# Cross attention of a perceiver block: a finished tile's out-projection one slot later, its norm in the next batch's first two slots

## What is computed

```python
xn = _ln(x, g_x, b_x)              # context, 16 x 512 x 512
ln = _ln(latents, g_l, b_l)        # latents, 16 x 64 x 512
q = ln @ w_q
k, v = jnp.split(concatenate([xn, ln], axis=1) @ w_kv, 2, axis=-1)
sim = jnp.einsum('bhid,bhjd->bhij', q, k)       # 8 heads of 64
attn = jax.nn.softmax(sim, axis=-1)
out = jnp.einsum('bhij,bhjd->bhid', attn, v)
x = x + _ln(out @ w_out, g_o, b_o)
```

## Time and profile before

| | |
|---|---|
| median of 3 runs | 982.22 us (981.43 to 985.5) |
| the profiled execution's own time | 984.02 us |
| its span, first to last instruction | 982.2 us |
| granted TensorE clock | 0.998 |
| busy share: TensorE, weight loads, VectorE, ScalarE, GpSimd | 97%, 79%, 78%, 45%, 13% |

### The profile page before, as it was taken

One profiled execution on the slowest core, in us unless ns is written; L12 is line 12 of the kernel. 1 busy time (PEld: TensorE's weight loads), 2 busy tenths in 40 slices (PEclk: granted clock), 3 DMA queues, 4 the chain that ended last, 5 costly groups with the idle time before them and its releaser, 6 DMA issues.

```text
span 982.2 us, 16675 instructions
## 1 busy us (share of the span) xinstructions
PE 948.5 (97%) x6400; PEld 778.0 (79%) x6400; DVE 768.8 (78%) x1647; ACT 439.4 (45%) x848; POOL 130.7 (13%) x145
## 2 busy tenths in 40 slices
PE   9999899998999999999999999999999999999997
PEld 7778788787887887887878888777676778888885
DVE  6546588788788988987887874568898598999985
ACT  4533664655465456547545654623333422222221
POOL 6420100101110100100111110023132100000000
PEclk9999999999999999999999999999999999999999
DMA  6687675956876685676758467081003940000000
GB/s 217 186 275 178 188 128 151 188 95 188 156 132 160 145 172 120 188 140 151 134 144 197 95 169 178 1 219 30 1 2 89 261 123 12 11 11 12 12 12 22
DMA packets 119451, 120.06 MB, mean 122 GB/s; under 512 B 47430, under 2 KB 88070, under 8 KB 117324
## 3 DMA queue, kind: packets, MB, share of 16 engines
q1 hardware_dynamic: 111980, 93.30, 35.8%
q0 software_dynamic: 6816, 24.64, 14.0%
q10 hardware_dynamic: 576, 1.05, 0.3%
HBM read 89.04 MB, written 29.93 MB: 121 GB/s over the span
## 4 chain that ended last, share of the span: by engine, by line
PE 57%; DVE 21%; DMA 10%; issue 5%; ACT 5%; SPq 1%; POOL 1%; another core or an unknown queue 0%; DVEq 0%; ACTq 0%
PE ps_banks L147 14%; PE ps_banks L148 13%; PE ps_banks L149 13%; DMA scratch_rstd<-sb_rstd_b 6%; PE ps_banks L472 4%; PE ps_banks L685 3%; DVE sb_kfull L928 3%; DVE sb_kT_lo L899 3%; DVE sb_b_stats L860 2%; PE ps_banks L752 2%; PE ps_banks L753 2%; PE ps_banks L604 2%; PE ps_banks L754 2%; DMA sb_rstd_row<-scratch_rstd 2%; DVE sb_wq_big L1055 1%
## 5 line engine op out<-in xcount | busy, mean ns | idle before, releaser
L1455 ACT ACTIVATE sb_kT_hi<-sb_kfull 128x512 fp32r<-128x512 f32 x64 | 40.5, 632 | 158.6 <-DVE sb_kfull L928 158.6
L147 PE MATMUL ps_banks<-sb_zT_hi,sb_wkv_hi 128*128 128x512 f32 x256 | 104.6, 409 | 0.4 <-DVE sb_kfull L928 0.2
L148 PE MATMUL ps_banks<-sb_wkv_lo,sb_zT_hi 128*128 128x512 f32 x256 | 100.3, 392 | 0.0
L149 PE MATMUL ps_banks<-sb_zT_hi,sb_wkv_lo 128*128 128x512 f32 x256 | 100.3, 392 | 0.0
L147 PE MATMUL ps_banks<-sb_wkv_hi,sb_zT_hi 128*128 128x512 f32 x256 | 100.1, 391 | 0.0
L149 PE MATMUL ps_banks<-sb_wkv_hi,sb_zT_lo 128*128 128x512 f32 x256 | 100.1, 391 | 0.0
L148 PE MATMUL ps_banks<-sb_zT_lo,sb_wkv_hi 128*128 128x512 f32 x256 | 99.9, 390 | 0.0
L979 DVE CUSTOM_DVE_ANT_0 sb_probs<-ps_banks,sb_maskbias 128x576 f32<-128x576 f32 x64 | 48.1, 751 | 33.4 <-PE ps_banks L149 32.7
L147 PE MATMUL ps_banks<-sb_wgu,sb_z_hi 128*128 128x512 f32 (+1 forms) x192 | 73.7, 384 | 0.0
L148 PE MATMUL ps_banks<-sb_wgu,sb_z_hi 128*128 128x512 f32 (+1 forms) x192 | 72.1, 376 | 0.0
L149 PE MATMUL ps_banks<-sb_wgu,sb_z_lo 128*128 128x512 f32 (+1 forms) x192 | 72.0, 375 | 0.0
(11 more groups left out here) (269 smaller groups left out, 2425.9 us busy)
## 6 DMA issues: line engine op xcount, KB each, us to landing
sb_ctx<-in_ctx SPq DMA_DIRECT2D x16, 1024.0 KB, 6.4
sb_ctxT<-in_ctx_t SPq DMA_DIRECT2D x16, 1024.0 KB, 8.6
scratch_wgu<-sb_w_both POOLq DMA_DIRECT2D x22, 512.0 KB
sb_wgu<-scratch_wgu SPq DMA_DIRECT2D x44, 256.0 KB, 5.1
sb_wdn<-scratch_wdn SPq DMA_DIRECT2D x8, 704.0 KB, 7.8
scratch_q<-sb_a_qk POOLq DMA_DIRECT2D x8, 512.0 KB, 6.7
sb_rstd_row<-scratch_rstd SPq DMA_DIRECT2D x16, 256.0 KB, 5.4
sb_qpack<-scratch_q SPq DMA_DIRECT2D x32, 128.0 KB, 8.4
```

The costliest lines, as they stand in the source:

```text
L147: e.matmul(o, wh, xh, start=i == 0, stop=False)
L148: e.matmul(o, wh, xl, start=False, stop=False)
L149: m = e.matmul(o, wl, xh, start=False, stop=i == n - 1)
L1455: e.activation(dst, src, ACT.Identity).then_inc(done)
```

## The change

The edits hold for tiles 0 to 6. The last tile (in the round that drains the loop) keeps its slots. TensorE's `project_out` goes from slot 6 to slot 7, after the scores of that slot and ahead of its values, and ScalarE's `copy_y` goes with it. VectorE's `out_stats` goes from the end of slot 7 to the end of slot 0 of the next batch, behind `scale_k`; `out_scale` goes from there to the end of slot 1. GpSimd's `power_one` goes from slot 7 to slot 0 of the next batch, behind the spill of that slot's weight, and `shift_y` to slot 1. No work is added or removed. `out_split` and `hi_of_attn` stay. The ring's order becomes: values 1, weight, probabilities 0, latent part 0, values 2, probabilities 1, latent part 1, y, values 3.

```diff
@@ tensor_program
-                    if b % 2 == 0 and b >= 2 and slot == 6:
+                    if b % 2 == 0 and b >= 2 and slot == (7 if cur else 6):
                         project_out((b - 2) // 2)
@@ vector_program
-                    if t_new is not None and slot == 7:
+                    if t_new is not None and not cur and slot == 7:
                         o_nth = out_stats(t_new)
                     if t_out is not None:
                         if slot == 0:
+                            o_nth = out_stats(t_out)
+                        if slot == 1:
                             out_scale(t_out, o_nth)
                         if slot == 7:
                             out_add(t_out)
@@ scalar_program
-                    if t_new is not None and slot == 6:
+                    if t_new is not None and slot == (7 if cur else 6):
                         copy_y(t_new)
@@ pool_program
-                    if t_new is not None and slot == 7:
+                    if t_new is not None and b == NB and slot == 7:
                         power_one(small_o, t_new)
                     if t_out is not None:
                         if slot == 0:
+                            power_one(small_o, t_out)
+                        if slot == 1:
                             shift_y(t_out)
                         if slot == 7:
                             power_one(small_y, t_out)
```

## The result

The changed kernel takes 996.35 us (median of 4 runs, 993.28 to 998.0) against 981.98 us (4 runs, 981.43 to 985.5). The ratio is 1.0113, 95% interval 1.0086 to 1.014: slower, by 11.1 us of 982 (8.4 to 13.8). The two medians lie further apart, 14.4 us, and with four executions of each this difference stays open; the forecast misses by either. Its profiled execution took 995.66 us with a span of 993.9, which is 11.7 us more than the span before. I had forecast + 6.2 us, 988.4, and the range to 992.0 does not hold the result.

The account below looks back on a forecast made before the run. The prediction took a slack-free two-batch loop through VectorE, the statistics' round trip and TensorE as the bound. It summed + 6.35 (odd runs) - 0.7 (TensorE's wait) + 0.5 (batch 13) = + 6.2 us, 988.4 us, range 980.0 to 992.0.

Parts of the forecast that it names:

- TensorE's wait: Slot 6, even batches: of 1.06 us, 0.23 gained and 0.83 left on copy_v; 0.7 us in all, bounds 0 and 1.2.
- Slot 0 gives nothing back: VectorE, odd batches: out_stats (1.02 us) replaces out_scale (1.27), but the next low half starts at 191.80 either way.
- `power_one` was hidden: GpSimd, slot 0: power_one, behind the spill, finishes before out_scale wants it, hidden by 0.26 us.
- the drain of the weight's bank: Transposes behind the moved project_v claim the turned weight's bank: no wait, with 0.2 us to spare.
- The rival of the new bank order: Slot 7's transposes wait for the bank if VectorE is 1 us later: five times 0.8, 992.4 us; chance 0.06.
- TensorE's second tie to the loop: Slot 1, even batches: transposes wait for a weight half whose buffer a spill frees, released by VectorE in odd slot 5.
- Slot 1: + 1.27 us: VectorE, odd batches: out_scale is new before L948, adding 1.27 us; five batches give 6.35 us, bounds 5.1 and 6.35.
- `shift_y` has until slot 7: 0: GpSimd's shift_y, moved to slot 1, is not needed until slot 7, so it costs 0.
- Batch 13: 0.5 us: Its later L948 makes VectorE 1.2 to 4.5 us late in batch 14; TensorE loses 0 to 3 us, 0.5 taken.
- The loop has no slack: Two-batch loop: VectorE's odd run (15.29 us), round trip (19.32), VectorE's even batch, TensorE's slots 6 and 7; no slack.
- What closes it: The statistics' round trip from L948 to scale_k: its 12.83 us store competes with traffic that L948 itself releases.
- the context columns' earlier issue: Even batches: 1 MB of columns issued sooner may delay the row's load up to 0.8 us each; 0 taken, 1.5 for range.

Follow-up runs that it names:

- The move alone: Kernel before with only project_out of tiles 0 to 6 and its copy_y moved to slot 7, VectorE and GpSimd as before: 971.2 us, ratio 0.9981.
- the kernel with `out_scale` first: Kernel before with project_out and copy_y in slot 7, out_stats ending slot 7, and out_scale ahead of scale_k in slot 0: 970.8 us, ratio 0.9979 to before.
- `shift_y` later: Changed kernel with GpSimd's shift_y in slot 5 instead of slot 1 of the odd batch: 977.01 us, ratio 1.0047 to the kernel before.
- `shift_y` beside L1040: Kernel before with one wait added, so that GpSimd's shift_y in slot 0 waits for the second scale_k: 978.39 us, ratio 1.0053.
- norm alone: Kernel before with only VectorE's and GpSimd's part of the diff, project_out staying in slot 6: 985.55 us, ratio 1.0126.
- With it short: Dense store, dense row load and scale_k reading with a stride of four: on the kernel before 979.41 us, ratio 1.0029; on the changed one 988.11, 1.0109.
- with TensorE slower: Dense store with TensorE taking every fourth column: on the kernel before 975.4 us, ratio 1.0030; on the changed one 976.01 us, 1.0034.

## Why the prediction was wrong

The direction and the place were right. One term of the sum was put at nothing and should have been nearly as large as the whole forecast; the move's gain and batch 13 were too small, and slot 1 was too large. In the prediction's order:

*TensorE's wait.* 1.06 us became 0.83 in batch 2, as derived, to 0.01 us. The move alone is worth 0.19% or 1.8 us (0.6 to 3.0); I had 0.7, bounds 0 and 1.2, so the two can't be told apart.

*Slot 0 gives nothing back.* Right, and shown by the kernel with `out_scale` first. `power_one` was hidden, and the drain of the weight's bank did not bite. The rival of the new bank order expected TensorE to wait for it in slot 7 of even batches, and no such wait came. The 6.4 us on the same line in the changed kernel stand elsewhere, at 224.6, 365.1, 436.3 and 576.0 us, about the start of batches 4, 8, 10 and 14. That is the wait that the prediction had called TensorE's second tie to the loop. With the move alone they are absent.

*Slot 1: + 1.27 us.* Measured by `shift_y` later: 16.25 - 15.29 = 0.96 us. `out_scale` takes 196.08 - 194.90 = 1.18 there, and L1035 behind it 0.68 instead of 0.92, since `shift_y` has left its side.

**"`shift_y` has until slot 7: 0."** This step failed. I asked when its result is wanted, and not what runs beside it. It costs 0.96 us per odd batch, in L1040: six times that is 5.8 us, about half of what the change costs, where the sum had 0. Taking it away gave 0.66%, 6.4 us; adding it alone, with a run of + 0.77, cost 0.53%, 5.2 us. The trace of before held the hint: L1035 at 0.92 us beside `shift_y`, where its neighbours of the same form take 0.68. The Trainium skill, "SBUF — State Buffer", section "SBUF: two separate sides", says that VectorE and GpSimd share a pair of ports which one instruction holds to its end, for VectorE's fast modes and for two inputs from SBUF. The trace agrees: L1040 ends 0.29 us after `shift_y`, and `shift_y`, which starts beside L1035, takes 1.66 us instead of 1.31.

*Batch 13: 0.5 us.* Batch 14 starts 578.50 - 542.93 = 35.57 us after batch 13, 31.88 before: VectorE is 3.7 us late, inside the 1.2 to 4.5 that I had derived. 1.8 of it are the run and 1.9 a later landing. From its last value matmul of batch 13 to that of batch 14 TensorE takes 37.41 us instead of 34.53: it loses 2.9 us. That is the upper end of my bounds of 0 and 3; I had taken 0.5 because this load had been short once.

*The loop has no slack.* Right upwards. Added run over the six odd batches against cost: 4.5 us cost 5.2 (`shift_y` beside L1040), 5.7 cost 6.4 (changed with `shift_y` late, against the move alone), 11.5 cost 12.3 (norm alone). Each passes on in full, within intervals of 1.3 to 2.3 us either way. Downwards TensorE's keys are 0.2 us behind.

*What closes it.* The prediction blamed the store's 12.83 us on the traffic that L948 releases. Wrong for most of it: without that load the spill takes 8 to 11 us, with 16-byte pieces 4 to 6. The rule on a strided last dimension that I had named (the Trainium skill, "DMA: Bandwidth & Descriptors", "Rules for kernel authors") is what the runs bear out: in longer pieces the store takes 4.4 us instead of 12.83, with 6144 packets fewer. The fixed 2 us of its "Anatomy" fit neither; the Trainium skill fitted them to DMAs issued by GpSimd, and this store is SyncE's. It changed no term of the sum. The trip is one of the ways in which the loop closes. With it short, VectorE's own list comes next, and the change still costs 0.8%; with TensorE slower, it costs 0.04%.

Sum by measured terms: + 11.4 (runs) - 1.8 (move) = + 9.6 us, of the 13.0 that TensorE is behind at the end of the loop in the two traces (11.7 at the end of the span). The other 3.4 us lie in round trips, which came out between 1.0 us shorter and 1.9 longer than in the trace of before: those behind batches 8 and 13 grew by 1.1 and 1.9. Their cause was not tested. I had named the context columns' earlier issue for it, up to 1.5 us, which stays open, and so does the part of the two stretches at half the clock. The profit of a short trip with neither side effect is open too: no kernel here had one. Nothing beats the kernel before by more than 0.23%, and the move alone brings 0.19% if the norm stays out of slot 1.

## What to carry to other kernels

Before moving an instruction on a lightly used engine, list what the busy engine will run beside it, and look in the trace for rows of one form with two durations: they price the neighbour. Work moved out of covered time into a run without idle rows cost its full length in each round of this loop; put ahead of the wait, where the idle time is, it cost nothing. Before shortening a wait in a loop, ask how far behind the next engine is: here it was 0.2 us. And when two traces are subtracted, compare the granted clock along them first: one stretch at half the clock made 1.6 us of difference here.

## What the hardware showed unexpectedly

- A 16-bit TENSOR_SCALAR on VectorE of 0.43 us takes 1.38 to 1.41 beside a GpSimd TENSOR_TENSOR of 128x512, one of 0.28 us takes 0.73 to 0.84: it ends 0.2 to 0.3 us after GpSimd's instruction. A float32 TENSOR_TENSOR with one input from PSUM (`scale_k`) keeps its 0.69 us beside the same instruction.
- Inside the loop, from its issue to that of the load that waits for it, a DMA of 512 single float32 numbers takes 8.2 to 13.6 us, one of the same bytes in pieces of 16 takes 3.8 to 5.7. A 1 MB load issued behind the first on the same engine's queue lands 13.8 us after its issue (median) instead of 6.4.
- Every fourth float32 column as a weight: 317 ns for a load of 128x128 instead of 188. The same stride in one SBUF input of VectorE's TENSOR_TENSOR: 1.03 to 1.11 us instead of 0.67 to 0.69.
- After TensorE had waited 1.96 us in batch 4, its granted clock was 0.50 (1.2 GHz) from 225.6 to 229.0 us, with matmuls 0.43 us apart instead of 0.23. By the end of that batch its lag behind the kernel before had fallen from 3.8 to 1.9 us.
